# Moving the row mixing of each batch behind the second large product

## The reference

```python
x = x + einsum('bct,bcd->bdt', x, w0[itok_0_15])        # mixes the 64 rows of a batch
x = x + einsum('bct,bcd->bdt', x, w1[itok_0_15])        # mixes them again, same index
low = einsum('bsi,bir->bsr', x, lora_A[itok_0_2])
x = x + einsum('bsi,oi->bso', x, W) + 0.5 * einsum('bsr,or->bso', low, lora_B)
x = x + einsum('bsi,boi->bso', x, w3[itok_3_7])         # a 1024x1024 matrix chosen for each batch
```

## Time and profile before

| | |
|---|---|
| median of 3 runs | 429.15 us (428.72 to 430.48) |
| span of the profiled execution | 426.4 us |
| runs above that span | 2.75 us (429.15 - 426.4) |
| TensorE busy with matmuls | 417.0 us, 98% of the span |
| VectorE, ScalarE, GpSimd busy | 162.1, 156.9, 9.0 us |

### The profile page before, as it was taken

The page is one execution under the profiler, slowest core; times in us unless marked ns, Lnnn a source line. Parts: engine busy times, 40 slices in busy tenths (PEclk is TensorE's granted clock), DMA queues, the critical chain, the costliest instruction groups (busy, mean ns, idle before and its releaser), DMA issues.

```text
span 426.4 us, 7365 instructions
## 1 busy us (share of the span) xinstructions
PE 417.0 (98%) x2032; PEld 354.1 (83%) x2032; DVE 162.1 (38%) x311; ACT 156.9 (37%) x237; POOL 9.0 (2%) x30
## 2 busy tenths in 40 slices
PE   8999999999999999999999999999999999999992
PEld 8988888888888888888888888888888888888881
DVE  3686697550015100041120569884136411261100
ACT  1576323423325232351320667573145211342100
POOL 1050010000000000000000000000000000000000
PEclk9799999999999999999999999999999999999998
DMA  8990224000321003430020289998208322032222
GB/s 256 323 363 4 74 76 136 13 1 28 122 86 63 0 2 101 137 134 0 2 98 2 98 296 373 354 309 281 52 2 261 88 52 46 8 76 51 53 54 52
DMA packets 22130, 48.26 MB, mean 113 GB/s; under 512 B 2165, under 2 KB 10485, under 8 KB 22070
## 3 DMA queue, kind: packets, MB, share of 16 engines
q1 hardware_dynamic: 19332, 39.07, 27.1%
q10 hardware_dynamic: 2738, 8.46, 7.7%
HBM read 39.13 MB, written 8.39 MB: 111 GB/s over the span
## 4 chain that ended last, share of the span: by engine, by line
PE 96%; DMA 1%; DVE 0%; ACT 0%; SPq 0%; issue 0%; ACTq 0%
PE ps L1014 42%; PE ps L942 14%; PE ps L943 14%; PE ps L944 14%; PE ps L906 7%; PE ps L963 4%; PE ps L971 2%; PE ps L895 1%; DMA xT<-w0t 1%; DVE xT L589 0%; PE ps L902 0%; ACT stage L506 0%; SPq L297 0%; ACTq L505 0%
## 5 line engine op out<-in xcount | busy, mean ns | idle before, releaser
L1014 PE MATMUL ps<-ring,aT 128*128 x784 | 178.0, 389 | 0.0
L1014 PEld LDWEIGHTS ps<-ring,aT 128*128 128x128 f32 x784 | 147.1, 188 | 30.7 <-issue 0.2
L942 PE MATMUL ps<-aT,ring 128*128 128x512 f32 x256 | 99.8, 390 | 0.0
L943 PE MATMUL ps<-aT,ring 128*128 128x512 f32 x256 | 99.7, 389 | 0.0
L944 PE MATMUL ps<-aT,ring 128*128 128x512 f32 x256 | 99.6, 389 | 0.0
L944 PEld LDWEIGHTS ps<-aT,ring 128*128 128x128 f32 x256 | 48.1, 188 | 10.1
L943 PEld LDWEIGHTS ps<-aT,ring 128*128 128x128 f32 x256 | 48.1, 188 | 9.8
L942 PEld LDWEIGHTS ps<-aT,ring 128*128 128x128 f32 x256 | 48.1, 188 | 9.4
L438 ACT ACTIVATE xT<-ps 128x512 f32<-128x512 f32 x32 | 18.6, 595 | 89.4 <-PE ps L944 74.7
L837 DVE TENSOR_TENSOR aT<-xT,aT 128x512 fp32r<-128x512 f32 (+1 forms) x36 | 22.2, 657 | 73.5 <-ACT aT L497 73.5
L497 ACT ACTIVATE aT<-xT 128x512 fp32r (+1 forms) x36 | 19.9, 599 | 72.8 <-PE ps L1014 72.1
(11 more groups left out here) (49 smaller groups left out, 192.5 us busy)
## 6 DMA issues: line engine op xcount, KB each, us to landing
raw<-w3t SPq DMA_DIRECT2D x24, 512.0 KB, 5.5
raw<-x SPq DMA_DIRECT2D x16, 512.0 KB, 3.6
aT_raw<-w3t SPq DMA_DIRECT2D x16, 512.0 KB, 6.3
out<-stage ACTq DMA_DIRECT2D x30, 256.0 KB, 3.3
xT<-wt SPq DMA_DIRECT2D x6, 512.0 KB, 6.9
a_raw<-lora_a SPq DMA_DIRECT2D x24, 128.0 KB, 2.0
xT<-lora_a SPq DMA_DIRECT2D x8, 128.0 KB, 4.8
raw<-wt SPq DMA_DIRECT2D x2, 512.0 KB, 6.7
```

Source lines behind the costliest of these rows:

```text
L942: pe.matmul(dst, unit(k, 0)[:, cs], aT[:, k, 0, :], start=start and k == 0, stop=False)
L943: pe.matmul(dst, unit(k, 0)[:, cs], aT[:, k, 1, :], start=False, stop=False)
L1014: last = pe.matmul(ps[i % 4][:, n, :], x3_split(i, k, start, P), ring[:, bass.ds(off + (part * D + n * 512), 512)], start=(k == 0 and j == 0),
```

## The change

The mixing moves from the front to the back. The host hands over `x` transposed (`xt`), so it is loaded straight into `xT` and split there; nothing of it is mixed before the products with W and w3. The 256 matmul instructions of line 906, the block-diagonal tiles, `mix_out` and the copies of line 600 and 376 go.

After slot i of the second large product, `rows_hi` (ScalarE) and `rows_lo` (VectorE) split its result straight from PSUM in two tiles of 64 high and 64 low rows, GpSimd puts the batch's matrix, split in high and low columns, into `st` (`mixers`), TensorE multiplies them (`mix(i)`, four matmuls of 512 columns), and the two halves of that result are added: ScalarE copies one (`mixed_cols`), VectorE adds the other (`mixed_sum`). The mixing of slot i stands in TensorE's queue behind the whole of slot i+1, and from slot 15 on behind its first half. Two PSUM tiles serve the slots in turn (four before).

Besides: `slot_lo` and the added identities of the adapters move from VectorE to GpSimd; all adapter tiles pass through the four `raw` buffers; the product with W has six PSUM banks for its outputs (three before); its first chunk runs o = 0 and 1 by halves of k; lora_B takes the place of the tables, after they are used, and stands in SyncE's queue behind all of W and the x of chunk 1; the tables are stored once, with a 128-partition layout; 26 warming matmuls of 256 columns stand for 14 of 128.

```diff
@@ sync (the new order of the loads)
             sp.dma_start(w1_s, w1).then_inc(s("w1"), 16)
+            sp.dma_start(w0_s, w0t).then_inc(s("w0"), 16)
             load_w(0)
+            for k in range(HALF):
+                load_x0(k)
             load_w(1)
+            for k in range(HALF, KT):
+                load_x0(k)
+            load_w(2)
+            load_w(3)
             sp.wait_ge(s("toks"), 16)
             for b in range(CB):
                 load_a(b)
+            for u in range(RAW, KT):
+                load_w(u)
             sp.dma_start(small[:, 0:C_SIZE], small_c).then_inc(s("consts"), 16)
             sp.dma_start(before, before_c).then_inc(s("consts"), 16)
+            load_x(1)
+            sp.wait_ge(s("mm"), 2)
+            sp.dma_start(b_raw, lora_b).then_inc(s("b_raw"), 16)
...
@@ gpsimd
+            adapter_eyes(0, 0)
+            word = slot_word(pool, 0)
+            slot_lo(0, word, (0, HALF))
+            slot_lo(0, word, (HALF, KT))
+            adapter_eyes(HALF, 0)
+            pool.wait_ge(s("tab_lo"), 1)
+            def step(i, word):
+                slot_lo(i + 1, following)
+                with pool.If(get(word, LOAD_A) > 0):
+                    adapter_eyes(0, pool.snap(get(word, THIS)))
+                mixers(i, word)
+                with pool.If(get(word, LOAD_B) > 0):
+                    adapter_eyes(HALF, pool.snap(get(word, THIS)))
...
@@ scalar
+            def rows_hi(i):
+                act.wait_ge(s("steps"), BEFORE3 + KT * (i + 1))
+                if i:
+                    act.wait_ge(s("mixed"), i)
+                for h in range(2):
+                    own = slice(h * T, (h + 1) * T)
+                    act.activation(r_tile(h)[own, :], acc(i)[own, :, :].rearrange("p a n -> p (a n)"), ACT.Copy)\
+                       .then_inc(s("r_hi"), 1)
             def step(i, earlier, word):
+                if i:
+                    rows_hi(i - 1)
                 slot_hi(i + 1, following)
-                if i:
-                    slot_out(i - 1, earlier)
                 for flag, place, t0 in ((LOAD_A, NEXT_A, 0), (LOAD_B, NEXT_B, HALF)):
+                    if i and t0:
+                        mixed_cols(i - 1, earlier)
                     with act.If(get(word, flag) > 0):
...
                             adapter_hi(t, in_two(ring[:, bass.ds(off + (t - t0) * UNIT, D)]), count8)
                 if i:
                     store(i - 1, earlier)
...
@@ vector
+            def rows_lo(i):
+                for h in range(2):
+                    own, other = slice(h * T, (h + 1) * T), slice((1 - h) * T, (2 - h) * T)
+                    dve.wait_ge(s("r_hi"), 2 * i + h + 1)
+                    dve.tensor_tensor(r_tile(h)[other, :], acc(i)[own, :, :].rearrange("p a n -> p (a n)"),
+                                      as_f32(r_tile(h)[own, :]), ALU.subtract).then_inc(s("r_lo"), 1)
+            def mixed_sum(i, word):
+                    for h in range(2):
+                        own = slice(h * T, (h + 1) * T)
+                        dve.wait_ge(s("cols"), 2 * i + h + 1)
+                        dst = stage[own, i % 2, :]
+                        dve.tensor_tensor(dst, mixed_ps[h][own, :, :].rearrange("p a n -> p (a n)"), dst, ALU.add)
...
@@ tensor
+            def mix(i, single):
+                pe.wait_ge(s("st"), 4 * (i + 1))
+                pe.wait_ge(s("r_lo"), 2 * (i + 1))
+                if i:
+                    pe.wait_ge(s("staged"), 2 * i)
+                def product(h, dst, start, stop):
+                    for n in range(2):
+                        last = pe.matmul(dst[:, n, :], st[:, i % 2, h, :], r_tile(h)[:, 512 * n:512 * (n + 1)],
+                                         start=start, stop=stop)
...
+            def slot(i, earlier, mine):
+                pe.wait_ge(s("s_lo"), 2 * i + 4 if i else 2)
+                if i >= 2:
+                    pe.wait_ge(s("r_lo"), 2 * (i - 1))
                 for half in range(2):
...
+                    if i and half == (i < LATE):
+                        mix(i - 1, earlier[2])
```

More of the change, by code:

```diff
@@ L380, in _ @@
+            for i in range(SURE):
+                word = step(i, word)
+            with contextlib.ExitStack() as nested:
+                for i in range(SURE, SLOTS):
+                    nested.enter_context(pool.If(n_slots > i))
+                    word = step(i, word)
         @block.scalar
@@ L556, in step, with last @@
                 return word, following
+            def last(i, word):
+                rows_hi(i)
+                mixed_cols(i, word)
+                store(i, word)
             earlier = None
@@ new lines, in mixed_sum @@
+            def mixed_sum(i, word):
+                single = get(word, SINGLE)
+                with dve.If(single < 1):
+                    for h in range(2):
+                        own = slice(h * T, (h + 1) * T)
+                        dve.wait_ge(s("cols"), 2 * i + h + 1)
+                        dst = stage[own, i % 2, :]
+                        dve.tensor_tensor(dst, mixed_ps[h][own, :, :].rearrange("p a n -> p (a n)"), dst, ALU.add)\
+                           .then_inc(s("staged"), 1)
+                with dve.If(single > 0):
+                    for n in range(2):
+                        dve.wait_ge(s("cols"), 2 * i + n + 1)
+                        dst = stage[0:T, i % 2, 512 * n:512 * (n + 1)]
+                        dve.tensor_tensor(dst, mixed_ps[0][0:T, n, :], dst, ALU.add).then_inc(s("staged"), 1)
@@ L855, in step @@
             def step(i, earlier, word):
                 following = slot_word(dve, i + 1) if i + 1 < SLOTS else None
-                if i + 1 < SURE:
-                    slot_lo(i + 1, following)
-                elif i + 1 < SLOTS:
-                    with dve.If(n_slots > i + 1):
-                        slot_lo(i + 1, following)
                 if i:
-                    single_sum(i - 1, earlier)
+                    rows_lo(i - 1)
                 for flag, place, t0 in ((LOAD_A, NEXT_A, 0), (LOAD_B, NEXT_B, HALF)):
+                    if i and t0:
+                        mixed_sum(i - 1, earlier)
@@ L869, in step, with last @@
                 return word, following
-            earlier = None
+            def last(i, word):
+                rows_lo(i)
+                mixed_sum(i, word)
+            earlier, word = None, slot_word(dve, 0)
             for i in range(SURE):
@@ L920, in mix @@
-            def mix(p):
-                wait_raw(pe, ("x", p))
-                pe.wait_ge(s("bd"), 2 * (p + 1))
-                if p >= CP + 2:
-                    pe.wait_ge(s("x2"), p - CP - 1)
-                if p % 2:
-                    pe.wait_ge(s("x3"), KT * (p // CP - 1) + 3)
-                for k in range(KT):
-                    last = mix_tile(p, k, ps_mix[p % 2][:, k // 4, P * (k % 4):P * (k % 4 + 1)])
-                last.then_inc(s("mixed"), 1)
+                pe.matmul(ps[3][:, 0, 0:2 * P], st[:, 0, 0, :], st[:, 0, :, :], start=True, stop=True)
@@ L932, in main @@
+            pe.wait_ge(s("w01i"), 2)
+            for g in range(2):
+                rows = slice(g * T, (g + 1) * T)
+                for c in range(NC_ // 2):
+                    last = pe.matmul(ps_low[:, g, T * c:T * (c + 1)],
+                                     w0_twice[rows, c, :, :].rearrange("p h n -> p (h n)"),
+                                     w1_s[rows, T * c:T * (c + 1)], start=True, stop=True)
+                last.then_inc(s("mm"), 1)
             def main(c, o, start, stop, tiles=(0, KT)):
@@ L933, in main @@
                 dst = ps_l2(c, o)
-                if start:
+                if start and tiles[0] == 0:
                     place_free(c, o)
```

518 lines of the change are left out of this document (206 added, 312 removed).

## The result

The changed kernel takes 477.63 us (median of 4 runs, 476.03 to 479.75) where the kernel before takes 429.46 (428.72 to 430.48): a ratio of 1.1125 [1.1083, 1.1166], 48 us slower. The forecast was slower, 454 us, with a range to 464: right in direction, too small by 24 us, and outside the range.

A forecast was written before the change was run, and what follows sets the result against it. TensorE bounds the kernel: start 20.6 + chunks 197.0 + slots 177.8 + mixing 14.5 + waits 24.6 + clock 1.5 + tail 15.3 = 451.3 us span, with 2.75 to runs 454. Likeliest 447 to 460, wider 438 to 464.

The forecast's parts named there:

- What bounds the kernel: Whole kernel: TensorE holds 96% of the chain, so only its work, start, end and new waits count.
- The start: Before the chunks: TensorE waits for late lora_B from about 32 to 39.2 us; chunk 0 begins as if at 20.6.
- GpSimd's price: In the slots: a 128x512 slot_lo subtraction on GpSimd takes 1.3 us, an identity of 128 columns 0.45.
- The order of the slots: Slot stage: the helpers' chain makes TensorE wait at slots 1, 3-6, 9, 10, 13-15, together 24.6 us, slot 4 most (6.5).
- The clock lowered after the long wait at slot 4: 1.5: Slot stage: lower TensorE clock behind the one long wait at slot 4 costs 1.5 us.
- The tail: After the last matmul: split, mixing, sum, stores and end take 15.3 us instead of 8.1.
- (a): Rival: GpSimd as fast as VectorE, start at 18, no lower clock: 440 us; chance 0.14.
- (b): Rival: GpSimd held by VectorE instructions with two SBUF inputs, 9 us more: 463 us; chance 0.13.
- (c): Rival: the slots' chain is hidden: 428 us, no change, or 421 with lora_B in time; chance 0.15.

The follow-up runs named there:

- Experiment 1: Changed kernel with lora_B loaded earlier in SyncE's queue, behind the LoRA matrices and ahead of the last four units of W: 463.26 us.
- experiment 2: Changed kernel with only slot_lo moved from GpSimd to VectorE, behind rows_lo: 463.83 us.
- Experiment 4: Changed kernel with dummy matmuls, whose result nobody reads, put into TensorE's known holes in the slots: 470.42 us.
- experiment 3: Changed kernel with ScalarE issuing the stores of slot i-2 behind slot_hi(i+1), without waiting for VectorE's fresh sum: 447.38 us.
- Kernel 8: Changed kernel with lora_B early, slot_lo on VectorE, stores one step later behind slot_hi, and LOAD_B conversions ahead of mixed_cols: 429.05 us.
- experiment 6: Changed kernel with the stores of slot i-2 issued at the old place, the end of the step, so only the wait for the sum goes: 452.89 us.
- 10: Changed kernel with lora_B early and the stores one step later behind slot_hi, slot_lo left on GpSimd: 440.86 us.
- 11: Changed kernel with lora_B early, stores one step later and LOAD_B conversions ahead of mixed_cols, slot_lo left on GpSimd: 437.99 us.
- 5: Changed kernel with LOAD_B's conversions ahead of mixed_cols and their low parts ahead of mixed_sum: 499.83 us.

## Why the prediction was right in direction and too small

**What bounds the kernel: right.** Every us lost is TensorE waiting, or its work behind a wait.

**The start: right, 3.6 us short.** TensorE reached the wait at 32.1 (forecast 32). lora_B was issued at 24.4, not 22, landed at 35.9, not 33.8, and TensorE stood 9.2 us, not 5 to 7, going on at 41.2 instead of 39.2. The restart then cost 2.7 instead of 1.6. Experiment 1 shows the place of the load to be the cause of the hole: 12.0 of its 14.3 us lie ahead of the slots. How long the hole is also depends on how soon TensorE gets there: in experiments 2 to 6, with the same loads, the matmuls after 10 us ran at half clock for 3.4 or 6.8 us, TensorE waited 5.4 to 8.5 us and went on at 40.1 to 41.2 all the same.

**GpSimd's price: right.** 32 subtractions of 128x512 took 1.283 us each (taken: 1.3); the split table was there 9.6 us into the slots (10.2), and slot_lo(1) began 1.4 us behind it, which the forecast left out; an identity took 0.50 in the mean (0.45). By the groups of experiment 2 VectorE does the same subtraction in 0.695 us. The Trainium skill, GPSIMD Engine Reference, section Performance versus the Vector engine, has GpSimd at about twice VectorE's time for such an operation. The traces agree, with 1.85.

**The order of the slots: right in where, short in how much.** Slots 1, 3, 4, 6, 9, 10, 13 and 15 waited, slot 4 longest (6.9, forecast 6.5). Slots 5 and 14 didn't wait, 8 and 12 did. The sum was 30.3, not 24.6. Two terms were left out. One is ScalarE's 1.46 us between steps. The other is TensorE's own start behind `slot_lo`: at slot 10 GpSimd's pair ended at 364.61 and the first product began at 365.35, 0.74 us later, and 0.75 at slots 6 and 13. With 1.46 us more on every turn of the chain, a delay behind a conversion is larger and is made up more slowly; that this explains the rest of the 5.7 us is argued, not shown slot by slot.

**The failed step: "The clock lowered after the long wait at slot 4: 1.5".** The mechanism is right and was given to one wait of ten; it cost 13.4 us in the slots. Not only the wait of 6.9 lowers the clock: it fell to 0.50 in six places, at slot 1 (a wait of 3.0 us), 4 (6.9), 6 (2.2 and 1.3), 10 (3.3 and 1.3), 13 (1.4, 0.8, 0.4 and 1.3 from slot 12 on) and 15 (5.0), for 3.4 or 6.8 us each. Experiment 4 shows that the clock is a cost of its own (7.2 us back by filling alone), and experiment 3 that it goes with the waits. A first size was to be had from before: the window of 10 to 20 us at a clock of 0.68, 6.4 us at half clock, was used for the start and not for the list of waits. The restarts of TensorE at full clock, 4.3 us, had no term at all. Together they are 17.7 us where the sum has 1.5, the largest part of the 26.7; the waits themselves (+5.7), the start (+3.6) and the tail (+1.2) are the rest.

**The tail: 16.5 against 15.3.** `mix` began 3.96 us after the last product (forecast 3.8), and took 1.25 instead of 1.0; the rest lies in the stores and the end behind the sum, 7.5 us instead of 6.8.

**The rivals.** (a), a fast GpSimd, fell with 1.283 us. (b), GpSimd held by VectorE, came to nothing for `slot_lo`, for the reason that the forecast gives against it: none of the 32 subtractions ran beside a VectorE instruction with two SBUF inputs. (c), the chain hidden, was wrong for the change as made. For the kernel without waits it has 428 with lora_B late and 421 with lora_B early. Kernel 8 has it early, so its 429.05 is to be held against the 421; that it lies at the other number is luck. Its slots begin at 211.3 as in that sum (14 + 197), but the stage keeps 5.2 us of waits and 2.2 of restarts, and the tail is 17.6 instead of 15.3, its mixing at half clock among it. The strongest single cause is the one that the forecast names in passing, "ScalarE waits for it in `store`": 25 us by experiment 6, 30 with the issues moved, the clock's share included (11.9 of the 32.4 that the slot stage gained). It was booked as 2.7 us a slot (5.0 - 2.3), which was thought to lie beside TensorE's work.

**What stays open.** How much of the lost clock a given wait brings isn't settled: the same wait ahead of slot 1 lowered it in five kernels and not in two others (below). Nor is the start: with lora_B early the slots began at 209.2 to 211.8 in six kernels with the same loads, and the clock was at 0.50 after 10 us for nothing, 3.4 or 6.8 us of it. So a difference of 2 us between two of these kernels need not be their edit. The single costs don't add up (58.3 singly, 42.4 together), so none of them is "the share" of its edit.

## What to carry to other kernels

A wait in an in-order queue that stands ahead of the next step's first link costs as a link of the chain, even one of 1.7 us as here: store what was finished a step ago, and the wait is gone. Price a hole of TensorE twice, once for its length and once for the work behind it at a lower clock, and expect a part of what a faster TensorE gives (a quarter to four tenths here) to go into waits while the other engines' chain is as long as a slot. An edit tried alone can lose where it gains in company (+22.2 us and -6.2 here), so mend the wait that uncovers it first, and judge the order after.

## What the runs showed of the hardware

**The clock behind a wait of some 3 us.** Seven kernels have a wait of 3.04 to 3.27 us ahead of slot 1. The 48 products behind it took 13.87 and 13.82 us in two (the changed kernel and 10), 12.78 to 12.81 in three (1, 6 and 11), and 11.20 in two (3 and 5). In kernel 3 the place looks like this in TensorE's timeline:

```profile
233.58 11.20 PE L938 MATMUL ps<-ring,aT 128*128 x48 [3.27 <-POOL aT L301]
```

A wait of 3.27 us, and no loss. So a wait of this length may cost 2.7 us more, 1.6 or nothing, and its length doesn't order the three.

**GpSimd beside VectorE.** Timeline of the kernel after, GpSimd and then VectorE:

```profile
350.93 1.23 POOL L312 CAST st<-aT 128x64 fp32r x1
```

```profile
349.43 3.81 DVE L757 TENSOR_TENSOR ring<-raw,ring 128x1024 f32 x3 [3.04 <-ACT ring L412]
```

A cast that takes 0.23 to 0.24 us alone takes 1.23 beside a VectorE subtraction with both inputs in SBUF, as in the earlier trace rows. An identity's addition took 0.45 to 0.47 us alone and up to 1.10 there. The 32 long subtractions (1.283 us in the mean) don't test it, since none ran beside such an instruction; 18 of them ran beside one that reads PSUM, at 1.27 to 1.30 us, the others took 1.26 to 1.29.

**ScalarE's queue.** Its DMA issues take 0.5 us each beside running activations (experiment 3). With a wait ahead of them they hold up what follows. Without one, but in front of `rows_hi`, they cost less, not nothing: kernel 6 is 5.5 us above kernel 3, some 4 without the difference at slot 1.
